# Moving projections, experts' choice and value products between the slots of a hybrid attention and mixture kernel

## The reference

```python
x = x + attn_a(layernorm(x))     # 16 heads of 8, rotary, causal, biases
x = x + ffn(layernorm(x))
x = x + attn_b(layernorm(x))     # as attn_a, with other weights and wavelengths
x = x + ffn(layernorm(x))

# ffn: 8 heads of 64, 5 experts, 2 of them chosen by head and token
q, k = x @ Wq, x @ Wk
gl_v, gl_o = x @ Ws, x @ Wd
wv = topk_mask(gl_v, 2) * sigmoid(gl_v)
v = einsum('bthe,btek->bhtk', wv, x @ Wv)
attn = softmax(q k^T / 8) v      # not causal
out = einsum('bthe,bthk,ekd->btd', topk_mask(gl_o, 2), attn, Wo)
```

## Time and profile before

| | |
|---|---|
| median of 3 runs | 2090.83 us (2090.65 to 2092.62) |
| the profiled execution | 2082.94 us, span of its instructions 2081.2 us |
| busy share of the span | PE 82%, DVE 78%, ACT 61%, POOL 51% |
| mean granted clock of PE | 0.933 |

### The profile page before, as it was taken

The page is one execution under the profiler, slowest core; times in us unless marked ns, Lnnn a source line. Parts: engine busy times, 40 slices in busy tenths (PEclk is TensorE's granted clock), DMA queues, the critical chain, the costliest instruction groups (busy, mean ns, idle before and its releaser), DMA issues.

```text
span 2081.2 us, 31948 instructions
## 1 busy us (share of the span) xinstructions
PE 1704.4 (82%) x10304; PEld 755.4 (36%) x10304; DVE 1619.6 (78%) x4088; ACT 1260.7 (61%) x2802; POOL 1051.5 (51%) x1124
## 2 busy tenths in 40 slices
PE   1557988889898888989888888989888898978775
PEld 0122433334343433434343433434333343434332
DVE  3647887888888888888889888888879888886451
ACT  0336758575675757566575757667585756657351
POOL 1224556463746656374555636465564637465433
PEclk8588999999999999999999999999999999999876
DMA  4121203011121212012120211112120211100000
GB/s 105 40 36 32 36 29 49 29 32 24 37 37 42 36 30 41 15 41 32 42 36 30 44 34 27 28 37 37 33 45 29 34 21 37 37 19 11 11 1 6
DMA packets 87364, 68.67 MB, mean 33 GB/s; under 512 B 10464, under 2 KB 82848, under 8 KB 87072
## 3 DMA queue, kind: packets, MB, share of 16 engines
q1 hardware_dynamic: 87200, 66.62, 15.3%
HBM read 32.51 MB, written 10.49 MB: 21 GB/s over the span
## 4 chain that ended last, share of the span: by engine, by line
PE 48%; DVE 34%; ACT 9%; issue 4%; POOL 2%; SPq 1%; DMA 0%; POOLq 0%; DVEq 0%; PEld 0%; PEldq 0%; ACTq 0%
DVE ztmp L964 5%; PE Y L471 5%; PE S1c L406 5%; DVE nmaxF L853 4%; DVE S1a L847 4%; PE S2a L436 4%; ACT Pq L690 4%; DVE S1b L847 4%; PE Y L462 4%; ACT PT L675 4%; DVE S1c L847 3%; PE M L601 3%; PE S1b L406 3%; PE M L564 3%; PE S1a L406 3%
## 5 line engine op out<-in xcount | busy, mean ns | idle before, releaser
L1075 POOL TENSOR_TENSOR Z<-Z,ztmp 128x1280 f32<-128x1280 f32 x112 | 324.8, 2900 | 325.8 <-DVE ztmp L964 324.6
L1042 POOL TENSOR_SCALAR_AFFINE_SELECT PT<-PT 128x256 f32<-128x256 f32 (+1 forms) x640 | 252.5, 406 | 390.9 <-ACT PT L675 387.1
L1066 POOL TENSOR_TENSOR Vf<-Vf,ztmp 128x512 f32<-128x512 f32 x256 | 348.9, 1363 | 106.1 <-DVE ztmp L936 97.5
L675 ACT ACTIVATE PT<-S2a 128x512 f32<-128x512 f32 x320 | 191.1, 597 | 238.3 <-PE S2b L428 188.7
L679 ACT ACTIVATE PT<-S2a 128x512 f32<-128x512 f32 x256 | 153.5, 600 | 211.8 <-PE S2a L436 209.9
L471 PE MATMUL Y<-PT,Vf 128*64 128x512 f32 x1024 | 274.8, 617 | 0.0
L936 DVE TENSOR_TENSOR ztmp<-xv,wv_s 128x512 f32<-128x512 f32 x256 | 231.8, 905 | 2.8 <-POOL Z L1075 2.8
L847 DVE CUSTOM_DVE_ANT_0 S1b<-S1b,maskw 128x128 f32<-128x128 f32 (+3 forms) x368 | 174.9, 507 | 73.3 <-PE S1c L397 69.8
L406 PE MATMUL S1c<-Kf,Qf 64*128 64x512 f32 x352 | 207.9, 672 | 28.8 <-ACT Pq L690 26.6
L406 PE MATMUL S1a<-Kf,Qf 64*128 64x512 f32 x352 | 206.8, 668 | 20.7 <-ACT Pq L690 20.7
L462 PE MATMUL Y<-PT,Vs 128*9 128x512 f32 (+3 forms) x2048 | 194.8, 455 | 0.0
(11 more groups left out here) (100 smaller groups left out, 3536.9 us busy)
## 6 DMA issues: line engine op xcount, KB each, us to landing
Qs<-parts SPq DMA_DIRECT2D x192, 64.0 KB
Ks<-parts SPq DMA_DIRECT2D x192, 64.0 KB
tab_s<-in_tab SPq DMA_DIRECT2D x16, 512.0 KB, 4.5
xr<-out_x SPq DMA_DIRECT2D x32, 256.0 KB, 2.9
out_x<-res SPq DMA_DIRECT2D x32, 256.0 KB, 2.2
wa_s<-in_wa SPq DMA_DIRECT2D x16, 320.0 KB, 3.1
xl<-out_x SPq DMA_DIRECT2D x16, 256.0 KB, 2.9
out_x<-in_x SPq DMA_DIRECT2D x8, 256.0 KB, 4.5
```

Of the source, the lines that this page charges most:

```text
L675: nc.scalar.activation(PT[:, slot % 2, b, :], t[:, :], ACT.Exp, scale=SCALE_A).then_inc(exps_done.sem, 1)
L1042: last = nc.gpsimd.affine_select(out=v, in_=v, compare_op=ALU.is_ge, fill=0.0, base=0, pattern=pattern, channel_multiplier=-1)
L1066: nc.gpsimd.tensor_tensor(Vf[:, i, :, :], Vf[:, i, :, :], vtmp[:, n % VBUF, :, :], ALU.add).then_inc(v_acc.sem, 1)
L1075: nc.gpsimd.tensor_tensor(Z[:, :, :, :], Z[:, :, :, :], ztmp[:, hh % 2, :, :, :], ALU.add).then_inc(z_acc.sem, 1)
```

## The change

Nothing is computed differently. Five things are placed elsewhere or done in another form:
- Projections: pair 0 stays at (6,8), pair 1 goes to (7,6), and pairs 2 and 3 to (0,6) and (1,6) of the next iteration. Their places in the bank tables move with them, and PE waits for each pair where its scores begin.
- Comparisons: from (6,7), (6,8) to (7,5), (7,6).
- Counting: two reductions of 800 elements become three sums of 16-bit tensors, over 640, 320 and 320 elements, at (7,7), (7,8), (7,9).
- The three steps of the sigmoid: from (7,1), (7,2), (7,9) to (0,2), (0,5), (0,9) of the next iteration.
- Value products: two in slot 1 and four in slot 2 become six in slot 2, at steps 0, 1, 3, 4, 6, 8.

The output products stay at (2,1).

```diff
         M0_USES = ["rows1",
...
-        M1_USES = ["YT6",
-                   "YT7", "ZT0", "ZT2",
+        M1_USES = ["YT6", "F q2",
+                   "YT7", "F q3", "ZT0", "ZT2",
...
-        F_STEPS = [(6, 8), (6, 9), (7, 6), (7, 8)]
-        V_STEPS = [(s, b) for s, bs in ((1, (8, 9)), (2, (1, 3, 5, 8)), (3, (0, 2, 4, 7)), (4, (0, 1, 3, 4, 5, 6, 7)),
-                                        (5, (0, 1, 2)))
+        F_STEPS = [(6, 8), (7, 6), (0, 6), (1, 6)]
+        V_STEPS = [(s, b) for s, bs in ((2, (0, 1, 3, 4, 6, 8)), (3, (0, 2, 4, 7)), (4, (0, 1, 3, 4, 5, 6, 7)), (5, (0, 1, 2)))
                    for b in bs]
...
-                    if group == SA and b == 0:
-                        pe.wait_ge(*drained(j, "F q3", 1))
-                        pe.wait_ge(*drained(j, "F k3", 1))
+                    if group >= SA and b == 0:
+                        for use in (f"F q{group - SA}", f"F k{group - SA}"):
+                            pe.wait_ge(*drained(j, use, 1 if group - SA < 2 else 0))
...
-                        if not f_prep:
+                        if not (f_prep if p < 2 else f):
...
-                            act.wait_ge(*filled(j, "F k3", 1))
+                            act.wait_ge(*filled(j, "F k3"))
...
-                        if at in F_STEPS and f_prep:
+                        if at in F_STEPS and (f_prep if at[0] > 5 else f):
...
-                def f_count(half):
-                    dve.wait_ge(pick_chain.sem, pick_chain.at(j, 1, 1))
-                    n = E * NT * HF
-                    by = beaten_by[:, :, :, :].rearrange("p e t g -> p (e t g)")
-                    beats = cmp_[:, :, :, :].rearrange("p b a g -> p (a g) b")
-                    with nc.allow_low_precision(reason="counts of at most 4 are exact in bfloat16"):
-                        nc.vector.tensor_reduce(by[:, n * half:n * half + n], beats[:, n * half:n * half + n, :],
-                                                AX.X, ALU.add).then_inc(pick_chain.sem, 1)
+                def f_count(step):
+
+                    by = beaten_by[:, :, :, :].rearrange("p e t g -> p e (t g)")
+                    dve.wait_ge(pick_chain.sem, pick_chain.at(j, step + 1, 1))
+                    if step == 0:
+                        nc.vector.tensor_tensor(cmp_[:, 0:2, :, :], cmp_[:, 0:2, :, :], cmp_[:, 2:4, :, :],
+                                                ALU.add).then_inc(pick_chain.sem, 1)
+                    else:
+                        nc.vector.tensor_tensor(cmp_[:, 0, :, :] if step == 1 else by, cmp_[:, 0, :, :],
+                                                cmp_[:, 1 if step == 1 else 4, :, :], ALU.add).then_inc(pick_chain.sem, 1)
...
-                        if at in ((6, 7), (6, 8)) and f_prep:
-                            for e in ((0, 1), (2, 3, 4))[b - 7]:
+                        if at in ((7, 5), (7, 6)) and f_prep:
+                            for e in ((0, 1), (2, 3, 4))[b - 5]:
                                 f_compare(e)
-                        if at in ((6, 9), (7, 0)) and f_prep:
-                            f_count(slot - 6)
-                        if at in ((7, 1), (7, 2), (7, 9)) and f_prep:
-                            f_sigmoid((1, 2, 9).index(b))
+                        if at in ((7, 7), (7, 8), (7, 9)) and f_prep:
+                            f_count(b - 7)
+                        if at in ((0, 2), (0, 5), (0, 9)) and f:
+                            f_sigmoid((2, 5, 9).index(b))
```

More of the change, by code:

```diff
@@ L153, in attention_and_mixture @@
         M0, M1 = pb("M0"), pb("M1")
-        M0_USES = ["rows1",
-                   "rows2", "ZT1", "F out",
-                   "rows3", "A xnT", "A qp",
+        M0_USES = ["rows1", "F k2",
+                   "rows2", "F k3", "ZT1",
+                   "F out", "rows3", "A xnT", "A qp",
                    "A kp",
-                   "A yNT", "F xnT", "F gate1", "F gate3", "F k0", "F k1",
-                   "rows0", "F k2", "F k3"]
-        M1_USES = ["YT6",
-                   "YT7", "ZT0", "ZT2",
+                   "A yNT",
+                   "F xnT", "F gate1", "F gate3", "F k0",
+                   "rows0", "F k1"]
+        M1_USES = ["YT6", "F q2",
+                   "YT7", "F q3", "ZT0", "ZT2",
                    "YT0", "A q",
@@ L167, in attention_and_mixture @@
                    "YT3", "A v", "A out",
-                   "YT4", "F gate0", "F gate2", "F q0", "F q1",
-                   "YT5", "F q2", "F q3"]
+                   "YT4", "F gate0", "F gate2", "F q0",
+                   "YT5", "F q1"]
         N_BANKS = [NA_B] * SA + [NF_B] * SF
@@ L235, in attention_and_mixture @@
         normA_chain = Signal("normA_chain", SA)
-        pick_chain = Signal("pick_chain", 6)
+        pick_chain = Signal("pick_chain", 7)
         mix_chain = Signal("mix_chain", 2)
@@ L710, in f_copies @@
                 def f_copies(p):
-                    act.wait_ge(expF_done.sem, expF_done.at(j, NF_B * (p + 1), 2))
+                    act.wait_ge(expF_done.sem, expF_done.at(j, NF_B * (p + 1), 2 if p < 2 else 3))
                     act.wait_ge(*filled(j, f"F q{p}"))
@@ L915, in f_sigmoid @@
                     if step == 0:
-                        dve.wait_ge(sig_e.sem, sig_e.at(j, 1, 1))
+                        dve.wait_ge(sig_e.sem, sig_e.at(j, 1, 2))
                         nc.vector.tensor_scalar(wv2, wv2, 1.0, None, ALU.add).then_inc(pick_chain.sem, 1)
                     if step == 1:
-                        dve.wait_ge(pick_chain.sem, pick_chain.at(j, 4, 1))
+                        dve.wait_ge(pick_chain.sem, pick_chain.at(j, 5, 2))
                         nc.vector.reciprocal(wv2, wv2).then_inc(pick_chain.sem, 1)
                     if step == 2:
-                        dve.wait_ge(pick_chain.sem, pick_chain.at(j, 5, 1))
+                        dve.wait_ge(pick_chain.sem, pick_chain.at(j, 6, 2))
                         wv3 = wv_s[:, :, :, :].rearrange("p e t h -> p (e t) h")
@@ L928, in f_value_product @@
                     if i == 0 and e == 0:
-                        dve.wait_ge(pick_chain.sem, pick_chain.at(j, 6, 2))
+                        dve.wait_ge(pick_chain.sem, pick_chain.at(j, 7, 2))
                         dve.wait_ge(y_filled.sem, y_filled.at(j, 1))
@@ L945, in f_mix_weights @@
                     dve.wait_ge(mix_chain.sem, mix_chain.at(j, 1, 2))
-                    dve.wait_ge(pick_chain.sem, pick_chain.at(j, 3, 2))
+                    dve.wait_ge(pick_chain.sem, pick_chain.at(j, 4, 2))
                     nc.vector.scalar_tensor_tensor(
```

## The result

| | before | after |
|---|---|---|
| median, same chip | 2090.74 us (2089.07 to 2092.62, 4 runs) | 2117.14 us (2114.73 to 2120.93, 4 runs) |
| ratio | 1 | 1.0133, 95% interval 1.0115 to 1.0151 |
| profiled execution (that of before is not one of the 4 runs) | 2082.94 us | 2120.93 us |
| mean granted clock | 0.933 | 0.924 |

The account below looks back on a forecast made before the run. PE and DVE were taken to alternate on the path, tied by three score banks. Slots: -2.3 - 0.4 + 4.2 - 1.0 = +0.5 us; with a clock fall 3.3, times 14 = 46: 2137 us, range 2120 to 2150, with rivals 2072 to 2178.

Parts of the forecast that it names:

- likeliest case: One clock fall an iteration, expected in slot 0: +2.6 to +3.9 us an iteration, 2127 to 2145 us; chance 0.38.
- another case: No clock fall in slot 0, today's in some iterations only: +0.5 to +2.4 us, 2098 to 2125 us; chance 0.17.
- Slot 6, -2.3 us: Slot 6: one projection pair stays at its end instead of two, and DVE loses comparisons and a reduction; 2.3 us gained.
- Slot 7, -0.4 us: Slot 7: reduction, add and reciprocal leave DVE, comparisons and sums enter, one comparison stalls about 1.4 us; 15.7 becomes 15.3.
- the wait of 2.39 us: Slot 7, step 8: DVE's wait for PE closes because the second projection pair (1.93 us) has left PE.
- Slot 0, the step that failed: Slot 0: added DVE work 1.45, stalled add 2.15, wait for projections 0.7, small corrections; +4.2 us before any clock fall.
- The add stalls for the 2.3 us that are left: Slot 0, step 2: POOL's Z addition starts 0.6 us ahead of the add, which stalls in nearly every iteration.
- 2.15 and 2.1 to 3.4 for the clock: Slot 0: 2.15 us for the add's stall, plus 2.1 to 3.4 for the clock fall after PE's idling.
- the prediction's own sign: Slot 0: the add lasts near 2.4 us in nearly every iteration; the prediction is wrong if it stays at 0.23.
- Slots 1 and 2, -1.0 us with the clock held: Two value products (1.2 us) leave slot 1; the products in slot 2 are charged 0.2; together -1.0 us at full clock.
- the faster rival: Slot 0's add does not stall, so the slot costs 2.0 instead of 4.2 us: 2067 to 2108 us; chance 0.20.
- theory 1: Follow-up theory: comparison and add stall behind POOL's Z addition, and PE's idle stretch behind each brings the clock down.

Follow-up runs that it names:

- e5: Kernel before with only the projections and their bank tables moved as in the change; comparisons, counting, sigmoid and value products as before: 2137.19 us, ratio 1.0261.
- e3: Changed kernel with the sigmoid's add at step 1 of slot 0 and the comparisons at steps 0 and 6 of slot 7: 2072.81 us, ratio 0.9951.
- e2: Changed kernel with the comparisons at steps 0 and 6 of slot 7, the add left at step 2 of slot 0: 2168.40 us, ratio 1.0416.
- e1: Changed kernel with the sigmoid's add one step earlier, at step 1 of slot 0: 2103.35 us, ratio 1.0100.
- e7: Changed kernel with the add at step 1, comparisons at steps 0 and 6 of slot 7, value products at their old steps: 2072.03 us, ratio 0.9951.
- e8: Kernel before with sums, comparisons at (7,0) and (7,6), sigmoid at steps 1, 5, 9 of slot 0; projections and value products as before: 2122.11 us, ratio 1.0192.
- e6: Kernel before with only the counting reductions replaced by sums, at (6,9) and (7,0): 2080.15 us, ratio 0.9992.

## Why the prediction was right, and where not

**The direction was right**, with its likeliest case (one fall an iteration, +2.6 to +3.9 us) against +3.43 measured. The time was 20 us too high, 3 us below that case's own range of 2120 to 2150, for two plain reasons. The 14 iterations counted are 38.0 / 3.43 = 11 in effect. And the 7.9 us that the median of before lay above its profiled execution did not recur: the median of after lies 3.8 below its own. The time lies in the range of another case, 2098 to 2125 (no fall in slot 0), whose condition did not hold: the clock fell at the start of slot 0 in every iteration.

Slot by slot the agreement is luck. By the marks of the prediction, slots 6 and 7 were forecast at -2.7 and measured at -3.0; slot 0 was forecast at +6.3 to +7.6 with its fall and measured at +3.0; the rest was forecast at -1.0 and measured at +3.4. Two errors of about 4 us cancel.

**Slot 6, -2.3 us**: measured -2.57 by the marks used there and -1.87 by PE's, which is its half of the projections; it was PE's slot, as said.

**Slot 7, -0.4 us**: right by the marks used there (15.3 us), with the comparison at 1.65 us against about 1.6 and the sums at 0.48 and 0.32 us against "0.4 to 0.5 and 0.25 to 0.3". These sums run at about twice the rate of a comparison, as the Trainium skill (VectorE: DVE Perf Modes, Mode 2×_1P) has it. One clause was wrong, that the wait of 2.39 us closes "because the second pair (1.93 us) has left PE": e5 has the wait unchanged. In after, and in e3 too, comparisons and sums stand in that time, and DVE does not wait.

**Slot 0, the step that failed.** "The add stalls for the 2.3 us that are left", in nearly every iteration. The mechanism is real, and so is its price: e2 has it in 14 of 16 iterations, e1 takes it away, and a bad iteration is 4.3 us longer in slot 0 than a common one, the low end of what 2.15 and 2.1 to 3.4 for the clock make. The 2.0 us that the slot was to cost without a stall were right too (by DVE's marks 10.8 to 12.7), with its wait of 0.7 us at step 8, which is 0.77 (at 532.68). But the order of add and Z addition is a race that the kernel after wins in 3 iterations of 4: the add takes 0.24 us in 8 of the 12 and 0.42 in one, and by the prediction's own sign ("wrong if the add stays at 0.23") it failed there. The prediction took PE to enter slot 0 at full clock with its masks early. It had itself priced the comparison's stall in slot 7, and did not ask what PE does meanwhile: it is idle for 2.0 us, and the clock falls. That fall stands in the place of the one that I gave to the add, but it costs nothing in slot 0 (e1: 13.71 us with it and without). So slot 0 costs +3.0 us in the mean instead of +4.2 plus 2.1 to 3.4 for the clock.

**Slots 1 and 2, -1.0 us with the clock held**: this failed as well, in two ways. The clock did not hold, and slot 1 costs +1.8 by PE's marks. And where it does hold the gain isn't there: the two value products that leave slot 1 were to be worth 1.2 us, but e3 without them and e7 with them both take 14.7 us in it. The products in slot 2 were charged 0.2 and cost 1.28 (e3 against e7, slots 2 and 3 where the clock holds: 18.32 and 14.45 against 17.72 and 13.77).

**The rule on who blocks whom** was right to lower the chance of the faster rival. The Trainium skill (SBUF — State Buffer, Who interferes with whom) has a tensor_scalar and a tensor_tensor of two SBUF inputs blocked for GpSimd's whole instruction; the trace agrees, with 2.98 us for the add, and with 1.65 for a comparison that came within such an instruction and ended with it. The rival itself had a true condition (the add must start before POOL's addition) and e1 met it, but the time it gave, 2067 to 2108, needed the 1.0 us of slots 1 and 2 and no more fall than today's; e1's 1.0100 would be 2112 us on the chip of the prediction.

**Still open** is what decides a fall of the clock. e7 shows the same slot with and without one, and e8 has the most low clock of all with no idle stretch of PE over 1.7 us. So the reading of the prediction, and of theory 1, that the longest idle stretch tells where the clock falls holds for the stretch of 2.0 us (behind it the clock fell in 12 iterations of 12 and 9 of 12, behind 0.96 at the same place in none of e3's), but it is no general rule. The falls in the slots of e6 and e8 whose instructions did not change were only seen, not explained.

## What to carry to other kernels

Where two engines are both full in a slot, price a move for the pair: half of this change alone cost 1.9 to 2.6%, and both halves, with two operations moved away from POOL's additions, gained 0.5%. When a step is found to stall, follow the engine that waits for it too, down to its clock, before costing the next slot. A short operation of the two kinds that stalled here (the add, a TENSOR_SCALAR, and the comparison, a TENSOR_TENSOR of two SBUF inputs) belongs directly behind the instruction whose end releases POOL, and not one bank later: 0.02 us decided over 2.7. And when a forecast comes out right in total, compare it slot by slot, by the same marks.

## What the runs showed of the hardware

A late engine can protect another: with the comparison's stall gone the add's stall appeared in 14 of 16 iterations, and the ratio rose from 1.013 to 1.042. The pattern of the granted clock can extend over several iterations: in e7 the fall in slot 0 comes in every third or fourth one, with equal work on DVE (12.67 and 12.69 us), so a single iteration doesn't price it. And less work on DVE can lengthen slots in which nothing was touched: e6 took 1.3 us out of slot 7 and lost them at low clock in slots 1, 3 and 4. Nor does a low clock always cost time: at the start of slot 0 it cost nothing, in slot 1 more than 1 us.
